# The self attention of a decoder block with its softmax normalised before the transposes

## The chip, the cores and the metric

The kernel runs on one core of a Trainium2 chip. The metric is the device time of one execution in microseconds; the time of a kernel is the median of its runs.

## The reference

One decoder layer on x (8 batches, 512 positions, 512 features), in fp32:

```python
x = x + attn(layernorm(x))          # this case: 16 heads of 64, causal, window 512, with scored global keys
x = x + cross_attn(ctx, layernorm(x), mask)
x = x + routed_ffn(layernorm(x))
# attn, h = rmsnorm(x) * norm_w:
q, k, v = h @ w_q, h @ w_k, h @ w_v
ll = where(causal, q k^T / 8, -1e30)               # local keys of the window
idx = top_k(h @ scorer_w + scorer_b, 128)          # global keys: their k and v are taken once more
lg = where(idx <= pos, q k[idx]^T / 8, -1e30)
a = softmax(concat(ll, lg)); o = a @ concat(v, v[idx]); return x + o @ w_out
```

As the window is the whole sequence, a chosen key counts twice in the softmax. The kernel never gathers: it ranks the scores and gives each chosen key the factor two.

## The kernel before

`self_attention` is one block with a program for each engine, and a loop over the 8 batches in each. The order of the work in a batch is a list written once by `attention_plan`; every engine walks it and does its own part of each entry, and semaphores carry the rest. So each engine's queue is in the order of the plan. Behind the self attention stand the cross attention and the feed-forward, which don't change.

A batch, in the plan's order. Each product of full precision is made of three products of rounded fp32 (high x high, low x high, high x low, `product`, L581 to L583).
- `v`: eight blocks of V = h w_v. ScalarE writes them to `vals` times `twice` (1 or 2 for each key, L381), and VectorE adds `twice` as a 65th column, so the values product also gives the row sum.
- `q`, `k`: a head pair's Q and K, 12 products of 512 columns each; ScalarE copies the high parts (Q once, K to both halves, L390 to L394), VectorE makes the low ones (L518, L522). Pair p + 1 is projected in the slots of pair p; pair 0 between the V blocks. All six weight parts stay in SBUF.
- Attention in slots g = 0 to 46. A head pair has five units of 512 score columns (`unit_blocks`). In slot g: `s` of unit g, `t` of unit g - 2, `pv` of unit g - 3.
- `s`: TensorE makes two score products and adds the causal mask with a bf16 product (L659 to L663) in one of two banks; VectorE takes the negated row maximum (L529, L534), ScalarE the exponential from PSUM to `probs` (L403).
- `t`: four fp32 transposes (L671), VectorE copies them to `probs_t` (L542).
- `pv`: fp32 products with the turned probabilities as the stationary operand and 65 columns of `vals` (L686, two passes each in the trace). VectorE inverts the row sum (L556) and scales the output (L557); `ot` transposes it (L695), ScalarE copies it to `o_t` (L411).
- `stats`, `dot`, `score`, `rank`: normalisation and ranking of the next batch, on VectorE and GpSimd; GpSimd's part (L323 to L337) makes scales from VectorE's statistics and scales `xb`. `ht`: `xb` turned for the next batch, after the last scores.
- `out`: four products of 8 fp32 matmuls (L710), each added to the residual on VectorE (L574) and stored. SP issues all loads and stores.

Ahead of the loop the weights are loaded in six parts of 1 MB in `W_ORDER`; ScalarE copies the high part (L366), VectorE subtracts for the low one (L481).

Of the kernel before, what the change touches and what calls it, by code (L numbers as in the profile page):

```python
# [18 lines left out]
F32 = mybir.dt.float32  # L19
# [5 lines left out]
ALU = mybir.AluOpType  # L25
# [59 lines left out]
def attention_plan():  # L85

    plan = [("v", i) for i in range(2 * TT - 2)] + [("q", 0), ("q_lo", 0), ("k", 0), ("k_lo", 0)]
    plan += [("v", i) for i in range(2 * TT - 2, 2 * TT)]
    for g in range(NU + 7):
        p, u = divmod(g, UNITS)
        if g < NU:
            plan.append(("s", g))
        if 2 <= g < NU + 2:
            plan.append(("t", g - 2))  # L100
        if 3 <= g < NU + 3:
            plan.append(("pv", g - 3))
        if g < NU and p + 1 < NPAIR and u < 4:
            plan.append((("q", "q_lo", "k", "k_lo")[u], p + 1))
        if g == 5:
            plan.append(("stats", 0))
        if g == 14:
            plan.append(("dot", 0))
        if g == 18:
            plan.append(("score", 0))  # L110
        if g in RANK_AT:
            plan.append(("rank", RANK_AT.index(g)))
# [14 lines left out]
def self_attention(nc, x, norm_w, w_q, w_k, w_v, w_out, scorer_w, scorer_b, x1):  # L127

    plan = attention_plan()
    PROJ, PT = bank_index(plan, ("v", "q", "k", "out")), bank_index(plan, ("t", "score", "ht", "ot"))  # L130
    with ExitStack() as ctx:
# [42 lines left out]
        twice = sb("twice", [P, TT])  # L174
        nmax = sb("nmax", [P, 4, 2])
# [70 lines left out]
        def _(sp):  # L246
# [1511 lines left out]
```

## Time and profile before

| | |
|---|---|
| time, median of 3 runs | 2299.57 us (2298.17 to 2301.93) |
| the profiled execution's own time | 2303.6 us |
| its span | 2301.9 us |
| mean granted TensorE clock | 0.945 of 2.4 GHz |
| TensorE busy | 2120.8 us, 92% |
| VectorE busy | 1320.5 us, 57% |
| ScalarE busy | 930.6 us, 40% |
| GpSimd busy | 343.7 us, 15% |

Busy times are of the whole span; the self attention takes the first two thirds of it. The profiled execution is one execution of the program, its span runs from the first to the last instruction. PE is TensorE, PEld its weight loads, DVE is VectorE, ACT ScalarE, POOL GpSimd, SP the engine that issues the DMAs. L574 is line 574 of the kernel before.

### The profile page before, as it was taken

What the parts mean: (1) busy time and instruction counts of PE and PEld (TensorE: products, weight loads), DVE (VectorE), ACT (ScalarE), POOL (GpSimd) and SP (SyncE); (2) the same over time, 40 slices, a digit from 0 to 9 for tenths busy, and PEclk for the clock granted to TensorE, in tenths of its full rate; (3) what the DMA queues carried; (4) which work ended last, traced back from release to release, by engine and by line L of the source; (5) the groups of instructions that cost most, each with busy time, mean ns of one, the idle gap of its engine ahead of it and who ended that gap; (6) DMA issues with size and microseconds to landing.
All of it is one profiled execution on the core that took longest, in us unless ns stands there. A gap on an engine that the chain in (4) does not pass through costs nothing. (4 is left out here: it accounts for less than half of the span.)

```text
span 2301.9 us, 36078 instructions
## 1 busy us (share of the span) xinstructions
PE 2120.8 (92%) x12029; PEld 1654.5 (72%) x12029; DVE 1320.5 (57%) x3145; ACT 930.6 (40%) x1989; POOL 343.7 (15%) x605
## 2 busy tenths in 40 slices
PE   3999999999999999999999999996899999978899
PEld 2886787688588688778868868864788888854543
DVE  5584376178167347537717826743787878745401
ACT  3442344244144244334415414424866666413210
POOL 2100100010010010001001001003554445320000
PEclk9999999999999999999999999996987878769899
DMA  5000000100100100000010010002013212150000
GB/s 192 1 2 33 24 1 13 44 1 1 56 1 1 55 3 1 27 31 1 11 47 1 1 57 1 1 33 81 27 59 133 61 58 67 51 201 1 1 0 19
DMA packets 46137, 80.24 MB, mean 35 GB/s; under 512 B 10067, under 2 KB 10067, under 8 KB 45448
## 3 DMA queue, kind: packets, MB, share of 16 engines
q1 hardware_dynamic: 45320, 75.85, 9.9%
q8 instruction: 103, 1.69, 0.3%
q0 software_dynamic: 640, 2.10, 0.2%
q14 instruction: 74, 0.61, 0.1%
HBM read 60.11 MB, written 17.83 MB: 34 GB/s over the span
## 5 line engine op out<-in xcount | busy, mean ns | idle before, releaser
L403 ACT ACTIVATE probs<-s_bank,nmax 128x512 f32<-128x512 f32 (+3 forms) x512 | 249.5, 526 | 368.5 <-DVE nmax L534 266.4
L686 PE MATMUL o_bank<-vals,probs_t 128*128 128x65 f32 x2560 | 329.0, 272 | 0.1
L686 PEld LDWEIGHTS o_bank<-vals,probs_t 128*128 128x128 f32 x2560 | 312.5, 192 | 13.1 <-DVE probs_t L542 12.9
L534 DVE TENSOR_REDUCE nmax<-s_bank 128x1 f32<-128x512 f32 (+2 forms) x384 | 184.4, 508 | 189.2 <-PE s_bank L663 186.5
L710 PE MATMUL pj_bank<-w_o,o_t 128*128 128x512 f32 x512 | 221.8, 594 | 6.0 <-ACT o_t L411 6.0
L542 DVE COPY probs_t<-pt_bank 128x512 f32<-128x512 f32 x320 | 217.8, 681 | 2.2 <-PE pt_bank L671 2.1
L671 PE MATMUL pt_bank<-ident,probs 128*128 128x128 f32 x1280 | 194.9, 275 | 15.7 <-DVE o_t L449 15.7
L659 PE MATMUL s_bank<-k_twice,q_both 128*128 128x512 f32 (+3 forms) x512 | 190.0, 373 | 2.1 <-DVE k_lo L522 2.1
L710 PEld LDWEIGHTS pj_bank<-w_o,o_t 128*128 128x128 f32 x512 | 96.6, 190 | 126.5 <-issue 126.5
L381 ACT ACTIVATE vals<-pj_bank,twice 128x512 f32<-128x512 f32 x64 | 43.9, 688 | 340.4 <-PE pj_bank L583 334.8
L518 DVE SCALAR_TENSOR_TENSOR q_both<-pj_bank,q_both 64x512 fp32r<-64x512 f32 x128 | 88.1, 688 | 141.7 <-ACT q_both L390 139.1
L661 PE MATMUL s_bank<-k_lo,q_both 128*128 128x512 f32 (+3 forms) x512 | 164.3, 321 | 0.0
L1255 PEld LDWEIGHTS x_o_bank<-vx,p_t 77*128 77x128 f32 x1024 | 148.0, 223 | 15.4 <-issue 5.4
L317 POOL TENSOR_TENSOR idle<-ones 128x4 f32<-128x4 f32 x41 | 8.1, 198 | 978.8 <-DMA probs<-in_x 976.7
L1071 ACT ACTIVATE e<-e,e_max 128x77 f32<-128x77 f32 x512 | 134.9, 351 | 33.3 <-DVE e_max L1130 33.3
L671 PEld LDWEIGHTS pt_bank<-ident,probs 128*128 128x128 f32 x1280 | 136.1, 142 | 16.5 <-issue 16.5
L1255 PE MATMUL x_o_bank<-vx,p_t 77*128 77x33 f32 x1024 | 143.4, 300 | 2.8 <-DVE att L1137 2.8
L574 DVE TENSOR_TENSOR probs<-pj_bank,probs 128x512 f32<-128x512 f32 x32 | 22.1, 691 | 212.1 <-PE pj_bank L710 199.8
L581 PE MATMUL pj_bank<-wv_hi,ht_hi 128*128 128x512 f32 x256 | 104.3, 407 | 22.8 <-ACT vals L381 9.9
L1020 POOL TENSOR_TENSOR e<-e,fill 128x616 f32<-128x616 f32 x64 | 95.4, 1491 | 187.3 <-DVE fill L1125 187.3
L663 PE MATMUL s_bank<-causal_b,ident_b 128*128 128x128 bf16 x512 | 118.0, 230 | 0.0
L1241 PE MATMUL e_bank<-qk_bd,xl_t 128*128 128x308 f32 x256 | 94.5, 499 | 23.3 <-DVE e L1119 22.6
(268 smaller groups left out, 4125.3 us busy)
## 6 DMA issues: line engine op xcount, KB each, us to landing
xb<-in_x SPq DMA_DIRECT2D x9, 1024.0 KB, 5.8
xt<-x SPq DMA_DIRECT2D x36, 256.0 KB, 2.8
probs<-in_x SPq DMA_DIRECT2D x32, 256.0 KB, 2.6
x<-probs SPq DMA_DIRECT2D x32, 256.0 KB, 2.0
am<-in_L_ffn_attention_mask SPq DMA_DIRECT2D x8, 1024.0 KB, 5.3
out<-x SPq DMA_DIRECT2D x32, 256.0 KB, 2.5
w_sb<-in_L_ffn_w SPq DMA_DIRECT2D x2, 4096.0 KB, 20.4
o_t<-in_L_attn_w_v SPq DMA_DIRECT2D x2, 1024.0 KB, 9.6
```

The costliest lines, as they stand in the source:

```text
L403: ins = nc.scalar.activation(probs[:, i % 2, c0:c0 + nk], s_bank[i % 2][:, c0:c0 + nk], ACT.Exp, bias=nmax[:, i % 4, n:n + 1])
L534: ins = nc.vector.tensor_reduce(nmax[:, i % 4, n:n + 1], s_bank[i % 2][:, c0:c0 + nk], AX.X, ALU.max, negate=True)
L542: nc.vector.tensor_copy(probs_t[:, i % 2, :], pt_bank[slot][:, :]).then_inc(ts_ready, 1)
L581: nc.tensor.matmul(out, lhs_hi, rhs_hi, start=start, stop=False)
L659: nc.tensor.matmul(s_bank[slot][:, c0:c0 + nk], both, k_twice[:, p % 2, h, 0:nk], start=True, stop=False)
L661: nc.tensor.matmul(s_bank[slot][:, c0:c0 + nk], both, k_lo[:, p % 2, h, 0:nk], start=False, stop=False)
L663: ins = nc.tensor.matmul(s_bank[slot][:, c0 + nk - P:c0 + nk], ident_b[:, :], causal_b[:, :], start=False, stop=True)
L671: ins = nc.tensor.transpose(pt_bank[slot][:, P * j:P * j + P], probs[:, i % 2, P * j:P * j + P], ident[:, :])
L686: ins = nc.tensor.matmul(o_bank[slot][:, o0:o0 + VW], probs_t[:, i % 2, c0 + P * kt:c0 + P * kt + P], vals[:, kt, 2 * p + h, :], start=(kt ...
L710: ins = nc.tensor.matmul(pj_bank[slot][:, :], o_t[:, c, P * i:P * i + P], w_o[:, c, :], start=(c == 0), stop=(c == NPAIR - 1))
L1071: ins = nc.scalar.activation(e[:, i % 4, h, :], e[:, i % 4, h, :], ACT.Exp, bias=e_max[:, i % 2, h:h + 1])
L1255: ins = nc.tensor.matmul(o_bank[:, VX * h:VX * h + VX], p_t[:, i % 2, h // CH, P * (h % CH):P * (h % CH) + P], vx[:, n.par, 2 * CH * (i % ...
```

## The change

The self attention is written anew in the same scheme of slots, three units to a head (512; 128 and 384; 256 columns), 48 units in a batch.
- Q is scaled by -1/8. VectorE adds a mask to the negated scores while it takes their minimum, and writes the sum to `probs`, a ring of four (`tensor_tensor_reduce`). The mask (`masks`, built once a batch by `build_masks` from a transposed row, entry `tw`) holds 1e30 for later keys and -ln 2 for chosen ones; the causal products and `twice` are gone.
- ScalarE takes the exponential from SBUF in place and accumulates the row sum (`den`). At the end of the next slot VectorE inverts it (`inverse`), and GpSimd multiplies the probabilities by it (`norm`); the transposes `t` are at g - 3.
- The turned probabilities are split: ScalarE copies the high part (`turned_hi`), VectorE subtracts for the low one (`turned_lo`). V is split in the same way, its low part beside the high one in `vals`.
- `pv`: once a head, eight products of rounded fp32 with 128 columns of `vals` (high and low) as the stationary operand and the turned probabilities as the moving one. The output comes out transposed; its two halves are added by a ScalarE copy (`o_raw`) and a VectorE addition (`o`). `ot` is gone.
- Projections of Q and K are cut in thirds of four products, one a slot; pair 0 of the next batch is projected in slots 50 to 55, `ht` moves to slots 46 to 49, `dot`, `score` and `rank` between the output products. `stats` is in slot 6.
- Split weights of Q and K no longer stay in SBUF: ahead of the loop SP stores them to device memory (`store_parts`), and each pair's 1 MB is loaded again per batch (`load_pair`). SP also moves K's high part to the other half by two DMAs (`move_k`), in place of ScalarE's copies.

Its core; removed lines stand in the functions above and are left out here:

```diff
+STEPS = (("o_raw", 8), ("k_high", 0), ("turned_hi", 3), ("norm", 1), ("s", 0), ("k_lows", 1), ("pv", 8), ("q_high", 0),
+         ("project", 0), ("q_low", 2), ("turned_lo", 4), ("t", 3), ("o", 9), ("inverse", 1))
+AHEAD, LAST_PAIR_AT, HT_AT, STATS_AT = 2, 50, 46, 6
...
+def unit_rows(u):
+    return ([(3, 0, 512)], [(0, 0, 128), (2, 128, 384)], [(1, 0, 256)])[u]
...
+thirds = {}
+for i in range(1, NPAIR + 1):
+    q0 = 2 * UNITS * (i - 1) - AHEAD if i < NPAIR else LAST_PAIR_AT
+    for j in range(3):
+        thirds[q0 + j] = ("q_third", 3 * i + j)
+        thirds[q0 + 3 + j] = ("k_third", 3 * i + j)
...
+plan = [("v", i) for i in range(2 * TT - 1)] + [("tw", 0), ("v", 2 * TT - 1)]
+for g in range(-AHEAD, LAST_PAIR_AT + 8):
+    for step, behind in STEPS:
+        n = g - behind
+        if step in ("norm", "s", "t", "turned_hi", "turned_lo", "inverse") and 0 <= n < NU:
+            plan.append((step, n))
+        if step in ("pv", "o_raw", "o") and n >= 0 and n % UNITS == 0 and n // UNITS < NH:
+            plan.append((step, n // UNITS))
+        if step == "project" and g in thirds:
+            plan.append(thirds[g])
+        if step in ("q_high", "q_low", "k_high", "k_lows") and last_third.get(n, " ")[0] == step[0]:
+            plan.append((step, last_third[n][1]))
...
+def store_parts(i):
+    n, hw = W_ORDER[i]
+    sp.wait_ge(split_lo, i + 1)
+    for part in range(2):
+        kind, r0 = 2 * (n == "k") + part, NPAIR // 2 * hw
+        if hw == 0:
+            for r in range(2):
+                sp.dma_start(w_pairs[r, :, kind, :], pair_part(i, r, part).rearrange("p c e -> p (c e)")
+                             .bitcast(F32)).then_inc(w_stored[i % 2], 16)
+        first = 2 if hw == 0 else 0
+        spare = (q_spare if i == 0 else p_spare)[part][:, DC * P * first:DC * P * (NPAIR // 2)]
+        sp.dma_start(w_pairs[r0 + first:r0 + NPAIR // 2, :, kind, :].rearrange("r p m -> p r m"),
+                     spare.rearrange("p (r m) -> p r m", m=DC * P).bitcast(F32)
+                     ).then_inc(w_stored[i % 2], 16)
...
+def move_k(b, i):
+    sp.wait_ge(k_hi_ready, i + 1 if b is None else b * NPAIR + i + 1)
+    for h in range(2):
+        own, other = head_rows(h), head_rows(1 - h)
+        sp.dma_start(k_twice[other, i % 2, h, :].bitcast(F32), k_twice[own, i % 2, h, :].bitcast(F32)
+                     ).then_inc(k_moved[i % 2], 16)
...
+def load_pairs(b, pairs):
+    for p in pairs:
+        if p > 2:
+            move_k(b, p - 2)
+        sp.wait_ge(k_low_ready, b * NPAIR + p - 1)
+        load_pair(p % NPAIR)
...
+if kind == "norm":
+    pl.wait_ge(den_ready, b * NU + i + 1)
+    for n, (_, c0, nk) in enumerate(unit_rows(i % UNITS)):
+        part = probs[:, i % RING, c0:c0 + nk]
+        ins = nc.gpsimd.tensor_tensor(part, part, rden[:, i % 4, n:n + 1].broadcast_to((P, nk)),
+                                      ALU.mult)
+    ins.then_inc(norm_ready, 1)
...
+if i == 3:
+    act.wait_ge(w_stored[0], STORED[0])
...
 if kind == "s":
     act.wait_ge(max_ready, b * NU + i + 1)
+    for n, (_, c0, nk) in enumerate(unit_rows(i % UNITS)):
+        part = probs[:, i % RING, c0:c0 + nk]
+        ins = nc.scalar.activation(part, part, ACT.Exp, bias=nmax[:, i % 4, n:n + 1], scale=-1.0,
+                                   accum_out=den[:, i % 4, n:n + 1])
     ins.then_inc(p_ready, 1)
+if kind == "turned_hi":
+    h, u = divmod(i, UNITS)
+    slot, ready = pt(b, ("t", i))
+    act.wait_ge(pt_ready, ready)
+    if u == 0 and h >= 2:
+        act.wait_ge(pv_ready, b * NH + h - 1)
+    n = len(TURN_ORDER[u])
+    nc.scalar.copy(p_hi[:, h % 2, TURNED_AT[u], :],
+                   pt_bank[slot][:, 0:P * n].rearrange("p (n k) -> p n k", k=P)).then_inc(hi_ready, 1)
...
+if kind == "o_raw":
+    act.wait_ge(pv_ready, b * NH + i + 1)
+    if i >= 2:
+        act.wait_ge(o_ready, b * NH + i - 1)
+    nc.scalar.copy(o_b[head_rows(i % 2), :], o_bank[i % 2][HD:P, :]).then_inc(ob_ready, 1)
...
+if i < 2:
+    dv.wait_ge(x1_out[i], b * (16 * TT // 2) + 1)
+elif i >= RING:
+    dv.wait_ge(pt_ready, pt(b, ("t", i - RING))[1])
+nc.vector.memset(carrier[:, 6 + i % 4:7 + i % 4], 0.0)
+m0 = MASK_AT[i % UNITS]
+for n, (_, c0, nk) in enumerate(unit_rows(i % UNITS)):
+    ins = nc.vector.tensor_tensor_reduce(
+        probs[:, i % RING, c0:c0 + nk], s_bank[i % 2][:, c0:c0 + nk],
+        masks[:, m0 + c0:m0 + c0 + nk], 1.0, 3e38, ALU.add, ALU.min, nmax[:, i % 4, n:n + 1])
 ins.then_inc(max_ready, 1)
...
+if kind == "inverse":
+    dv.wait_ge(p_ready, b * NU + i + 1)
+    n = len(unit_rows(i % UNITS))
+    nc.vector.reciprocal(rden[:, i % 4, 0:n], den[:, i % 4, 0:n]).then_inc(den_ready, 1)
+if kind == "turned_lo":
+    h, u = divmod(i, UNITS)
+    slot, _ = pt(b, ("t", i))
+    dv.wait_ge(hi_ready, b * NU + i + 1)
+    n = len(TURN_ORDER[u])
+    nc.vector.tensor_tensor(p_lo[:, h % 2, TURNED_AT[u], :],
+                            pt_bank[slot][:, 0:P * n].rearrange("p (n k) -> p n k", k=P),
+                            p_hi[:, h % 2, TURNED_AT[u], :].bitcast(F32),
+                            ALU.subtract).then_inc(lo_ready, 1)
+if kind == "o":
+    dv.wait_ge(ob_ready, b * NH + i + 1)
+    rows = head_rows(i % 2)
+    nc.vector.tensor_tensor(o_t[rows, i // 2, :], o_bank[i % 2][0:HD, :], o_b[rows, :],
+                            ALU.add).then_inc(o_ready, 1)
...
+def project(b, kind, i, thirds):
+    slot, _ = pj(b, (kind, i))
+    hi, lo = (w_qk[:, i % 2, 2 * (kind == "k") + k] for k in range(2))
+    for n in range(4 * thirds[0], 4 * thirds[-1] + 4):
+        c, form = divmod(n, 3)
+        w, moving = ((hi, ht_hi), (lo, ht_hi), (hi, ht_lo))[form]
+        ins = nc.tensor.matmul(pj_bank[slot][:, :], w[:, c, :], moving[:, c, :], start=(n == 0),
+                               stop=(n == 3 * DC - 1))
+    if thirds[-1] == 2:
+        ins.then_inc(pj_ready, 1)
...
 if kind == "s":
+    h, u = divmod(i, UNITS)
+    p = h // 2
+    if h % 2 == 0 and u == 0:
+        pe.wait_ge(q_lo_ready, b * NPAIR + p + 1)
+        pe.wait_ge(k_low_ready, b * NPAIR + p + 1)
+        pe.wait_ge(k_moved[p % 2], b * (32 * NPAIR // 2) + 32 * (p // 2 + 1))
     if i >= 2:
+        pe.wait_ge(max_ready, b * NU + i - 1)
+    for t, c0, nk in unit_rows(u):
+        both = q_both[:, p % 2, h % 2, P * t:P * t + P]
+        nc.tensor.matmul(s_bank[i % 2][:, c0:c0 + nk], both, k_twice[:, p % 2, h % 2, 0:nk],
                          start=True, stop=False)
+        ins = nc.tensor.matmul(s_bank[i % 2][:, c0:c0 + nk], both, k_low[:, p % 2, h % 2, 0:nk],
                                start=False, stop=True)
     ins.then_inc(s_ready, 1)
 if kind == "t":
     slot, _ = pt(b, (kind, i))
+    pe.wait_ge(norm_ready, b * NU + i + 1)
     pt_empty(b, (kind, i))
+    for j, k in enumerate(TURN_ORDER[i % UNITS]):
+        ins = nc.tensor.transpose(pt_bank[slot][:, P * j:P * j + P],
+                                  probs[:, i % RING, P * k:P * k + P], ident[:, :])
     ins.then_inc(pt_ready, 1)
 if kind == "pv":
     if i == 0:
+        pe.wait_ge(v_lo_ready, b * (2 * TT) + 2 * TT)
+    pe.wait_ge(lo_ready, b * NU + UNITS * i + UNITS)
     if i >= 2:
+        pe.wait_ge(o_ready, b * NH + i - 1)
+    parts = [(p, k) for p in (p_hi, p_lo) for k in (0, 3, 1, 2)]
+    for n, (part, k) in enumerate(parts):
+        ins = nc.tensor.matmul(o_bank[i % 2][:, 0:P * (TT - k)], vals[:, k, i, :],
+                               part[:, i % 2, KEYS_AT[k], :], start=(n == 0),
+                               stop=(n == len(parts) - 1))
     ins.then_inc(pv_ready, 1)
```

## Rows read from the trace of the kernel before

**Rows 1.** Windows view: length, busy time and count of each engine, granted clock, DMA.
```profile
422.10:451.20 29.10, 28.19 (x122) 22.66 (x122) 2.99 (x6) 8.39 (x14) 0.00 (x0) 1.00 0.15 46
451.20:583.20 132.00, 127.89 (x892) 110.06 (x890) 101.27 (x245) 63.02 (x119) 8.87 (x20) 0.99 0.01 5
478.97:495.15 16.18, 16.18 (x114) 13.90 (x113) 11.02 (x26) 7.88 (x15) 0.00 (x0) 1.00 0.00 2
```

**Rows 2.** Output additions (L574) of batch 0 and of batch 7.
```profile
L574 DVE TENSOR_TENSOR probs<-pj_bank,probs x4: 692/692/692, 212.8 to 233.3; 128x512 f32<-128x512 f32 x4
...
L574 DVE TENSOR_TENSOR probs<-pj_bank,probs x4: 691/691/691, 1532.6 to 1553.2; 128x512 f32<-128x512 f32 x4
```

**Rows 3.** TensorE's timeline, projections: start, duration, line; first and last of 95.
```profile
422.50 0.40 PE L582 MATMUL pj_bank<-wv_hi,ht_lo 128*128 128x512 f32 x1
...
443.83 0.39 PE L583 MATMUL pj_bank<-ht_lo,wk_hi 128*128 128x512 f32 x1
```

**Rows 4.** TensorE's timeline, two attention slots without a projection.
```profile
566.26 0.48 PE L659 MATMUL s_bank<-k_twice,q_both 128*128 128x512 f32 x1
566.57 0.40 PE L661 MATMUL s_bank<-k_lo,q_both 128*128 128x512 f32 x1
566.81 0.23 PE L663 MATMUL s_bank<-causal_b,ident_b 128*128 128x128 bf16 x1
566.88 0.60 PE L671 MATMUL pt_bank<-ident,probs 128*128 128x128 f32 x4
567.32 1.00 PE L686 MATMUL o_bank<-vals,probs_t 128*128 128x65 f32 x8
568.13 0.31 PE L659 MATMUL s_bank<-k_twice,q_both 128*128 128x128 f32 x1
...
568.43 0.42 PE L659 MATMUL s_bank<-k_twice,q_both 128*128 128x384 f32 x1
568.69 0.34 PE L661 MATMUL s_bank<-k_lo,q_both 128*128 128x384 f32 x1
568.87 0.23 PE L663 MATMUL s_bank<-causal_b,ident_b 128*128 128x128 bf16 x1
```

**Rows 5.** VectorE: two groups by form, and two steps of its timeline.
```profile
L522 DVE TENSOR_TENSOR k_lo<-pj_bank,k_twice 64x512 fp32r<-64x512 f32 x128 | 87.7, 685 | 22.7 <-ACT k_twice L394 19.9 <-issue 1.8
...
L556 DVE RECIPROCAL o_rden<-o_bank 128x2 f32<-128x2 f32 x192 | 31.3, 163 | 3.0 <-PE o_bank L686 2.0
...
498.15 0.69 DVE L440 SCALAR_TENSOR_TENSOR o_t<-xb,sw 128x512 f32<-128x512 f32 x1
...
498.89 0.69 DVE L440 SCALAR_TENSOR_TENSOR o_t<-xb,sw 128x512 f32<-128x512 f32 x1
```

**Rows 6.** ScalarE, the exponential's widest form.
```profile
L403 ACT ACTIVATE probs<-s_bank,nmax 128x512 f32<-128x512 f32 x128 | 88.2, 689 | 118.6 <-DVE nmax L534 110.4 <-PE pt_bank L671 3.3
```

**Rows 7.** GpSimd and VectorE side by side, timeline; and one line's durations (min/median/max).
```profile
16.58 2.29 DVE L481 TENSOR_TENSOR wv_lo<-o_t,wv_hi 128x2048 fp32r<-128x2048 f32 x1 [0.28 <-ACT wv_hi L366]
16.71 5.06 POOL L337 TENSOR_SCALAR xb<-xb,st 128x512 f32<-128x512 f32 x4
...
468.88 0.20 POOL L323 TENSOR_TENSOR st<-mv,eps_ln 128x4 f32<-128x4 f32 x1 [53.59 <-DVE mv L428]
...
473.89 3.03 POOL L337 TENSOR_SCALAR xb<-xb,st 128x512 f32<-128x512 f32 x4
...
1717.58 1.49 POOL L1020 TENSOR_TENSOR e<-e,fill 128x616 f32<-128x616 f32 x1 [6.53 <-DVE fill L1125]
1717.65 0.42 DVE L1137 TENSOR_TENSOR att<-x_o_bank,att_den 128x256 f32<-128x256 f32 x1
...
L1024 POOL TENSOR_TENSOR x<-xt,att x64: 721/730/1178, 1599.0 to 2000.8; 128x256 f32<-128x256 f32 x64
```

**Rows 8.** Before the first batch: ScalarE's timeline, and a load of weights (us to landing).
```profile
48.93 1.27 ACT L381 ACTIVATE vals<-pj_bank,twice 128x512 f32<-128x512 f32 x2 [5.62 <-DVE wk_lo L481]
...
o_t<-in_L_attn_w_q SPq DMA_DIRECT2D x2, 1024.0 KB, 5.1
```

More of the change, by code:

```diff
@@ L117, in attention_plan @@
-    plan.append(("ot", NPAIR - 1))
-    plan += [("out", t) for t in range(TT)]
+    thirds = {}
[4 more added lines that the diff above has]
+            thirds[q0 + 3 + j] = ("k_third", 3 * i + j)
+    last_third = {g: (kind[0], n // 3) for g, (kind, n) in thirds.items() if n % 3 == 2}
+    plan = [("v", i) for i in range(2 * TT - 1)] + [("tw", 0), ("v", 2 * TT - 1)]
@@ L124, in bank_index, with self_attention @@
     return {s: i for i, s in enumerate([s for s in plan if s[0] in kinds])}
-def self_attention(nc, x, norm_w, w_q, w_k, w_v, w_out, scorer_w, scorer_b, x1):
+def self_attention(nc, x, norm_w, w_q, w_k, w_v, w_out, scorer_w, scorer_b, w_pairs, x1):
     plan = attention_plan()
-    PROJ, PT = bank_index(plan, ("v", "q", "k", "out")), bank_index(plan, ("t", "score", "ht", "ot"))
+    PROJ = bank_index([(kind[0], i // 3) if kind.endswith("third") else (kind, i) for kind, i in plan
+                       if not kind.endswith("third") or i % 3 == 2], ("v", "q", "k", "out"))
+    PT = bank_index(plan, ("t", "score", "ht", "tw"))
     with ExitStack() as ctx:
@@ L182, in self_attention @@
         w_loaded, split_hi, split_lo = [sem(f"w_loaded{i}") for i in range(2)], sem("split_hi"), sem("split_lo")
+        w_stored, pair_in = [sem(f"w_stored{i}") for i in range(2)], [sem(f"pair_in{i}") for i in range(2)]
         small_in, wo_in, x_in = sem("small_in"), sem("wo_in"), sem("x_in")
@@ L464, in rank, with build_masks @@
                     step(nc.vector.tensor_tensor(cnt[:, 0, :], cnt[:, 0, :], cnt[:, 1, :], ALU.add))
-                    if b is not None:
-                        dv.wait_ge(v_ready, n * (2 * TT))
-                    nc.vector.tensor_scalar(twice[:, :], cnt[:, 0, :], TOPK - 0.5, 1.0, ALU.is_lt,
-                                            ALU.add).then_inc(twice_ready, 1)
+                    nc.vector.tensor_scalar(chosen[:, :], cnt[:, 0, :], TOPK - 0.5, -LN2, ALU.is_lt,
+                                            ALU.mult).then_inc(chosen_ready, 1)
+            def build_masks(b):
+                slot, ready = pt(b, ("tw", 0))
+                dv.wait_ge(pt_ready, ready)
+                row = pt_bank[slot]
+                for at, n in ((0, 3), (640, 2), (1024, 1)):
+                    done.mark(nc.vector.tensor_copy(masks[:, at:at + P * n], row[:, 0:P * n]))
+                for at, k in ((384, 3), (512, 0), (896, 2), (1152, 1)):
+                    ins = nc.vector.tensor_tensor(masks[:, at:at + P], row[:, P * k:P * k + P], later_keys[:, :], ALU.add)
+                done.wait(dv)
+                ins.then_inc(masks_ready, 1)
             def normed(b, n, c):
@@ L623, in _ @@
                 transposed(None, 0, c)
+            pe.wait_ge(ht_lo_ready, DC)
+            pe.wait_ge(split_lo, 1)
+            project(None, "q", 0, range(3))
+            pe.wait_ge(split_lo, 2)
+            project(None, "k", 0, range(3))
             score_rows(None, 0)
```

432 lines of the change are left out of this document (206 added, 226 removed).

## The prediction

> **What bounds the kernel now.** I read the windows view over one batch of the self attention first. The projection of V takes 29.1 us, the attention stretch 132.0 us, and in the latter TensorE is busy 127.9 us, VectorE 101.3, ScalarE 63.0 and GpSimd 8.9; over one head pair of 16.18 us TensorE is never free and VectorE is busy 11.0 [rows 1]. So TensorE's own issue order sets the time. The period of a batch follows from the first output addition of batch 0 at 212.8 and of batch 7 at 1532.6: 1319.8 / 7 = 188.5 us [rows 2]. The eight periods end near 1554 us; the cross attention and the feed-forward behind them, 748 us, are not touched by the diff. Then I took the prices of TensorE's work from its timeline: 94 steps of a 512-wide product from 422.50 to 443.83, so 0.227 us each or 0.443 ns a column [rows 3]; and one slot without projection, 1.87 us: scores 0.62 (the last 0.07 is the causal product), four transposes 0.44, probabilities by values 0.81 [rows 4].
>
> **What the change removes from TensorE.** Per head, after: score products 1.5 us (the same 2 x 1280 columns; 0.31 + 0.24 for the 512-wide pair, 0.26 for the 128-wide one, 0.45 for the 384-wide one, 0.33 estimated for 256 [rows 4]); ten transposes at 0.11, 1.1 us, as before; the values product as eight products of 512, 128, 384, 256 columns twice, 2560 x 0.443 ns = 1.13 us, and 1.3 with the 128-wide ones costing 0.13 more than their columns [rows 3, 4]; projections 12 x 0.227 = 2.7 us. Sum 6.65 us a head, 13.3 a pair, against 16.18 [rows 1]. Gone are the causal products (some 0.2 a head), 0.7 of 2.05 us on the values product, and the transposes of the output.
>
> **What it adds to VectorE.** Durations end to start overlap a little, so I use spacings. The masked minimum (a two-input operation that reads PSUM and a mask and returns a row value) is in no row. Its lower bound is a plain pass, 0.61 us for 512 columns, the upper one two cycles an element, +0.53 us on 512; the nearest row is the multiply with an accumulated sum, 0.74 us from start to start [rows 5]. I take that: 0.74, 0.34, 0.61 and 0.47 for 512, 128, 384, 256 columns, 2.16 a head (1.95 to 3.5). Three memsets and three reciprocals 0.6 (the reciprocal is 0.16 [rows 5]); the low parts of the turned probabilities 0.65 + 0.65 + 0.39 = 1.7, like any 512-wide pass; the output addition 0.7; the low parts of Q and K 1.4 a head, as now (0.685 each, [rows 5]). Sum 6.55 us a head. VectorE goes from 68% of the pair to 98% of TensorE's new 6.65: the two are level, and what I predict hangs on that.
>
> **ScalarE and GpSimd.** ScalarE takes over the high copies of the turned probabilities (1.3 us a head) and the upper half of the output (0.5) beside the exponentials (2.1 at 0.69 for 512 columns [rows 6]) and two copies of Q and K a head (1.0). The accumulated row sum is shown nowhere on ScalarE; nothing to 0.2 us for each of four, I take 0.1. About 5.3 us a head, 80%, covered by TensorE. The normalisation on GpSimd: 616 columns take 1.49, 256 take 0.73 [rows 7], so 1.28, 1.5 and 0.77 us for the three units, 3.6 a head. It waits for the reciprocal at the end of VectorE's next slot and is wanted at the end of TensorE's slot three: more than a slot (2.2 us) of room, so free, except in one place.
>
> That place is slot 6. VectorE takes the next batch's statistics there (2.9 us now), and GpSimd then works them off, 468.88 to 476.92, 8.0 us with the four scalings that begin at 473.89 [rows 7]. Now nothing is behind that in GpSimd's queue; afterwards the normalisation of unit 6 is, then 7 and 8. In slots from the first third: TensorE ends slot 5 at 11.4, VectorE starts slot 6 at 12.0 and ends it with the statistics at 16.2; GpSimd is free at 24.3, unit 6 is normalised at 25.7, its transposes end at 26.2 instead of 19.9. TensorE can do nothing else in between: 6.3 us a batch lost. The granted clock is 1.00 and 0.99 of the upper level in these stretches [rows 1]; what such a stall does to it no row of them shows, and I leave it to the range.
>
> **Port.** VectorE's subtraction with both inputs in SBUF, 2.29 us at 16.58 ran beside GpSimd's four scalings, which took 5.06 us; four of the same at 473.89 took 3.03, with no such operation beside them. At 1717.58 GpSimd's product took its usual 1.49 us while VectorE ran a PSUM-and-SBUF product of 0.42 [rows 7]. The added VectorE work is of this last form, so I add nothing. The Trainium skill (SBUF — State Buffer, "SBUF: two separate sides") says that GpSimd and VectorE share a port pair as an exclusive lock, taken by a VectorE operation with two SBUF inputs; by this rule the added operations, with one input in PSUM, don't collide, and the trace agrees. Read more broadly, as if any two-input operation took the lock, the rule would give the last rival below.
>
> **One batch.** Fill and the statistics, to the end of slot 9: 26.2 us. Slots 10 to 39, five pairs, at 13.3 plus 3% for waits between two level engines, 13.7: 68.5. Slots 40 to 47 have no projection; VectorE sets them, 8/3 x 5.15 = 13.7, less 0.9 that TensorE is ahead. Slots 48 on: turned probabilities and the next batch's transposes alternate in two banks and each waits for ScalarE and VectorE, 2 x 2.3, then the last products and six thirds of a projection, 8.3: 12.9. Sum 120.4. The V stage is 96 x 0.227 = 21.8, with the wait for the last addition 0.9 and one row of transposes for the mask 0.45: 23.2. The first Q and K, 5.4 us of it now, have moved into the slots. The output products stay 27.5. Together 171.1 against 188.5: 17.4 us a batch, 139 in eight.
>
> **Before the first batch.** ScalarE's first copy of V starts at 48.93 and waits for the last weight split [rows 8]. Now the weights are written to memory in between: the fifth part is split until some 43.8, its store of 2 MB (5.1 us for 1 MB [rows 8], so 7.5 estimated) lands at 51.5, the last part is copied and split in 5.2 us, to 56.5, and its store holds ScalarE until 64. That is 15 us later. SP carries more too: two SBUF-to-SBUF moves and a 1 MB load a pair. The move of K is issued some 1.1 us after the last third's end and is wanted 4.8 us after that slot. No row shows such a move: the 1 MB load at 5.1 us [rows 8] is its upper bound, and up to 3.7 us it fits. I take it as fitting; at the bound it costs 1.4 us in seven pairs, 10 us a batch. Behind it in SP's queue stand only the next pair's load, wanted 14 us later, and at the end of a batch the stores of the output.
>
> **The sum.** Profiled execution 2303.6 (span 2301.9 and 1.7 around it) + 15 - 139 = 2180; the median of the runs is 4 us under the profiled one, so 2176.
>
> **Rivals.**
> - *TensorE alone sets the time*: statistics fit in, no loss at slot 9. Batch 164.8, 8 x 23.7 = 190 off, 2125. For it: the other engines' sums are all below 6.65. Against it: GpSimd's queue is in order. Chance 0.15.
> - *Waits between the engines*: the K move lands late, or row sums on ScalarE cost 0.2 each, and a pair takes 15.0. Six to eight such pairs make 7.5 us a batch: 2236. For it: four engines hand each unit on, at 80 to 98% each. Chance 0.22.
> - *Slower, through the masked minimum*: at two cycles an element VectorE needs 6.55 + 1.33 = 7.9 us a head, 21.3 more a batch, 192.4 in all: +31 + 15, 2346. It decides from where the batch has lost 15.5 us, 1.0 a head or 0.25 us on each such operation. For it: no row shows it. Against it: accumulating rows run at one element a cycle. Chance 0.13.
> - *GpSimd and VectorE exclude each other*: 3.5 us a head more, 56 a batch, about 2620. The product at 1717.58 speaks against it. Chance 0.04.
> - *The bound isn't where I see it, no change*: 0.03.
>
> My forecast has 0.43; its own range is 2140 to 2215. 0.2% (4.6 us) is about what a measurement of this kernel tells from no change. Faster 0.80, within 0.03, slower 0.17. From the first rival to beyond the second the range is 2110 to 2270.
>
> **What would show it.** A period between first output additions of 170 to 172 us; TensorE's steady pair at 13.3 to 13.9 with VectorE over 93% busy; one idle stretch of TensorE of 4 to 7 us a batch, released by GpSimd, some 20 us after the V stage; masked minimum 0.69 to 0.77 us for 512 columns; the normalisation 1.2 to 1.35; ScalarE's first copy of V near 64. I am wrong if VectorE's minimum is above 1 us, if GpSimd's products are longer than 1.5 us at 512 columns, or if the score products wait for the K move in each pair.

## The result, and the profile after

The changed kernel takes 2241.03 us (median of 4 runs, 2240.01 to 2247.91) against 2299.46 for the kernel before, measured beside it: a ratio of 0.9751, with an interval of 0.9730 to 0.9772. It is faster, by 58 us; 123 were forecast. Its profiled execution spans 2238.0 us.

The page of the changed kernel: span, busy time by engine, granted clock in 40 slices.

```profile
span 2238.0 us, 34486 instructions
...
PE 1966.6 (88%) x9781; PEld 1515.5 (68%) x9781; DVE 1410.7 (63%) x4171; ACT 1114.9 (50%) x2837; POOL 705.8 (32%) x1116
...
PEclk9899999999999999999999999988888878678899
```

The output additions (L716 now) of batch 0 and batch 7, which answer to [rows 2]:

```profile
L716 DVE TENSOR_TENSOR probs<-pj_bank,probs x4: 690/691/692, 221.5 to 242.5; 128x512 f32<-128x512 f32 x4
...
L716 DVE TENSOR_TENSOR probs<-pj_bank,probs x4: 691/692/692, 1468.5 to 1489.5; 128x512 f32<-128x512 f32 x4
```

The period is (1468.5 - 221.5) / 7 = 178.1 us; it was 188.5 and should have become 171.1. So 10.4 us a batch came in and 7.0 are missing, 56 of the 60 us between the profiled execution (2240.0) and its forecast (2180). Of the rest, 2.6 are in front: the first copy of V starts at 66.63, not 64. The medians lie 65 us apart, not 60, because the forecast took off 4 us from the profiled execution to its median, and this one lies 1 us below its median. The stretch behind the eight periods is 748 us long, as before.

The windows view of batch 2, which answers to [rows 1]: V; slots to 8; slot 9 with a stall; the three slots behind it; slots to 39; 40 to 46; the tail to the first output product; the output. The last line is one steady head pair. Columns: length; busy time and count of PE, PEld, DVE, ACT, POOL; clock; DMA share; GB/s.

```profile
421.50:443.80 22.30, 22.26 (x100) 18.46 (x101) 6.43 (x14) 4.11 (x7) 0.00 (x0) 1.00 0.32 107
443.80:461.90 18.10, 17.49 (x96) 14.61 (x95) 14.46 (x58) 12.54 (x33) 6.84 (x11) 1.00 0.23 74
461.90:470.50 8.60, 2.73 (x14) 2.12 (x13) 4.02 (x12) 2.99 (x8) 7.73 (x17) 0.82 0.13 31
470.50:478.20 7.70, 7.70 (x36) 6.62 (x35) 4.55 (x16) 4.33 (x12) 3.00 (x5) 0.76 0.41 134
478.20:536.40 58.20, 58.20 (x348) 50.64 (x347) 52.75 (x184) 48.78 (x127) 25.49 (x36) 1.00 0.29 92
536.40:549.00 12.60, 9.73 (x62) 7.31 (x60) 11.99 (x48) 11.77 (x33) 6.27 (x10) 1.00 0.35 105
549.00:571.00 22.00, 16.29 (x81) 13.61 (x82) 9.48 (x19) 9.16 (x19) 4.69 (x8) 0.84 0.07 25
571.00:599.10 28.10, 27.11 (x67) 11.88 (x65) 13.97 (x34) 0.41 (x1) 2.28 (x6) 1.00 0.18 58
...
484.67:497.50 12.83, 12.83 (x78) 11.15 (x77) 11.61 (x41) 10.78 (x28) 5.66 (x9) 1.00 0.32 104
```

The steady pair is better than forecast: 12.83 us, TensorE never free. The time is lost at its two ends, around 465 and from 536 on. TensorE's waits say for what:

```profile
PE pt_bank L835 <- DVE p_lo L693: 59.8, 40, 2.3
PE pt_bank L835 <- POOL probs L435: 48.8, 16, 5.9
```

Each row gives a total in us, how often, and the longest. The second is the stall that was forecast at 6.3 us a batch. Its timeline in batch 2:

```profile
465.54 3.02 POOL L420 TENSOR_SCALAR xb<-xb,st 128x512 f32<-128x512 f32 x4
468.52 2.75 POOL L435 TENSOR_TENSOR probs<-probs,rden 128x512 f32<-128x512 f32 x4
469.61 1.11 PE L835 MATMUL pt_bank<-ident,probs 128*128 128x128 f32 x4 [5.87 <-POOL probs L435]
470.38 0.46 PE L825 MATMUL s_bank<-k_twice,q_both 128*128 128x128 f32 x1
```

GpSimd scales the next input, then normalises the units that have piled up, and TensorE has stood for 5.87 us. The four transposes behind it take 1.11 us where they take 0.60 to 0.66 in the steady slots, and the granted clock over the next 7.7 us is 0.76: it starts at the lower level, 1.2 GHz (0.50), and is 1.00 again from 475.0 on.

The first row of waits was not in the forecast as such. A stretch of the tail, timeline of four engines:

```profile
552.29 0.41 PE L835 MATMUL pt_bank<-ident,probs 128*128 128x128 f32 x2 [1.10 <-DVE p_lo L693]
552.54 0.60 PE L753 MATMUL pt_bank<-ident,xb 128*128 128x128 f32 x4
552.74 0.37 ACT L517 CAST p_hi<-pt_bank 128x256 fp32r<-128x256 f32 x1 [0.94 <-PE pt_bank L835]
553.51 0.68 ACT L451 ACTIVATE ht_hi<-pt_bank,nw 128x512 fp32r<-128x512 f32 x1
554.22 0.75 DVE L596 SCALAR_TENSOR_TENSOR ht_lo<-pt_bank,nw,ht_hi 128x512 fp32r<-128x512 f32 x1 [2.00 <-ACT ht_hi L451]
554.88 0.41 DVE L693 TENSOR_TENSOR p_lo<-pt_bank,p_hi 128x256 fp32r<-128x256 f32 x1
555.44 0.63 PE L835 MATMUL pt_bank<-ident,probs 128*128 128x128 f32 x4 [2.31 <-DVE p_lo L693]
```

The input of `p_lo` (`p_hi`) was there at 553.11, but `ht_lo` of the slot before stands ahead of it in VectorE's queue and waits for ScalarE until 554.19. Only then is `p_lo` made, and TensorE gets its bank back at 555.4.

### The profile page after: what moved, and what is told of

Its sections match the earlier page's. It is cut to its first block and busy times, and to the rows that moved or that the text cites. A ratio compares the mean times of both kernels' runs of the same rounds, so it can differ in the third digit from the quotient of the medians.

```text
span 2238.0 us, 34486 instructions
## 1 busy us (share of the span) xinstructions
PE 1966.6 (88%) x9781; PEld 1515.5 (68%) x9781; DVE 1410.7 (63%) x4171; ACT 1114.9 (50%) x2837; POOL 705.8 (32%) x1116
## 5 line engine op out<-in xcount | busy, mean ns | idle before, releaser
L435 POOL TENSOR_TENSOR probs<-probs,rden 128x512 f32<-128x512 f32 (+3 forms) x512 | 361.5, 720 | 733.1 <-DVE rden L687 732.1
L775 PE MATMUL pj_bank<-ht_hi,w_qk 128*128 128x512 f32 x1040 | 351.5, 402 | 1.6 <-DVE ht_lo L596 1.6
L507 ACT ACTIVATE probs<-probs,nmax 128x512 f32<-128x512 f32 (+3 forms) x512 | 286.6, 562 | 26.3 <-DVE nmax L680 26.0
L517 ACT CAST p_hi<-pt_bank 128x512 fp32r<-128x512 f32 (+1 forms) x384 | 197.3, 514 | 195.5 <-PE pt_bank L835 191.4
L680 DVE CUSTOM_DVE_ANT_0 probs<-s_bank,masks 128x512 f32<-128x512 f32 (+3 forms) x512 | 240.5, 488 | 10.4 <-issue 10.1
L693 DVE TENSOR_TENSOR p_lo<-pt_bank,p_hi 128x512 fp32r<-128x512 f32 (+1 forms) x384 | 229.7, 598 | 17.9 <-ACT p_hi L517 14.7
L775 PEld LDWEIGHTS pj_bank<-ht_hi,w_qk 128*128 128x128 f32 x1040 | 198.8, 194 | 32.7 <-DVE ht_lo L596 2.0
L775 PE MATMUL pj_bank<-ht_lo,w_qk 128*128 128x512 f32 x520 | 207.8, 400 | 0.0
L827 PE MATMUL s_bank<-k_low,q_both 128*128 128x512 f32 (+3 forms) x512 | 167.3, 327 | 0.0
L723 PE MATMUL pj_bank<-wv_hi,ht_hi 128*128 128x512 f32 x256 | 102.1, 399 | 32.9 <-DVE vals L660 23.1
L660 DVE TENSOR_TENSOR vals<-pj_bank,vals 128x512 fp32r<-128x512 f32 x64 | 44.1, 691 | 135.4 <-ACT vals L497 135.4
```

Source lines behind the costliest of these rows:

```text
L435: ins = nc.gpsimd.tensor_tensor(part, part, rden[:, i % 4, n:n + 1].broadcast_to((P, nk)), ALU.mult)
L507: ins = nc.scalar.activation(part, part, ACT.Exp, bias=nmax[:, i % 4, n:n + 1], scale=-1.0, accum_out=den[:, i % 4, n:n + 1])
L517: nc.scalar.copy(p_hi[:, h % 2, TURNED_AT[u], :], pt_bank[slot][:, 0:P * n].rearrange("p (n k) -> p n k", k=P)).then_inc(hi_ready, 1)
L680: ins = nc.vector.tensor_tensor_reduce(probs[:, i % RING, c0:c0 + nk], s_bank[i % 2][:, c0:c0 + nk], masks[:, m0 + c0:m0 + c0 + nk], 1.0, ...
L693: nc.vector.tensor_tensor(p_lo[:, h % 2, TURNED_AT[u], :], pt_bank[slot][:, 0:P * n].rearrange("p (n k) -> p n k", k=P), p_hi[:, h % 2, TU ...
L775: ins = nc.tensor.matmul(pj_bank[slot][:, :], w[:, c, :], moving[:, c, :], start=(n == 0), stop=(n == 3 * DC - 1))
```

## Experiments

Each kernel's ratio is to the kernel before, run on the same chip; the brackets are 95% intervals. Differences from the changed kernel are against 2241.

**The two halves of the stall at slot 9.** e1 takes the statistics of the next input (VectorE's and GpSimd's part) out of slot 6 and puts them between blocks of V:

```diff
-    plan = [("v", i) for i in range(2 * TT - 1)] + [("tw", 0), ("v", 2 * TT - 1)]
+    plan = [("v", i) for i in range(2 * TT - 4)] + [("stats", 0)] + [("v", i) for i in range(2 * TT - 4, 2 * TT - 1)]
+    plan += [("tw", 0), ("v", 2 * TT - 1)]
...
-        if g == STATS_AT:
-            plan.append(("stats", 0))
```

> The statistics of the next batch (VectorE's part and GpSimd's) move from slot 6 into the V stage, behind the fourth V block. If GpSimd's queue order is what holds TensorE in slot 9, the 5.9 us wait and the some 2 us of half clock behind it go in each of eight batches: about 63 us off the changed kernel's 2241, 2178. If the waits have another source (VectorE level with TensorE), TensorE waits elsewhere and no more than 20 us go.

Measured 2177.64, ratio 0.9462 [0.9429, 0.9495]: 63 us faster than the changed kernel, 7.9 a batch, as expected. Of TensorE's 48.8 us of waits for GpSimd at the transposes 1.8 are left, and in batch 2 TensorE works without a gap from 444 to 456 us, in slot 9 (its scores start at 445.06) and behind it, at a clock of 1.00; the waits for `p_lo` stay, 59.9 us. e2 moves VectorE's half alone; GpSimd's part stays in slot 6.

```diff
+    plan = [("v", i) for i in range(2 * TT - 4)] + [("bn", 0)] + [("v", i) for i in range(2 * TT - 4, 2 * TT - 1)]
...
-                    if kind == "stats":
+                    if kind == "bn":
                         stats(b + 1)
```

> Only VectorE's statistics move into the V stage; GpSimd's 8 us of work on them stays in slot 6, ahead of the normalisation. If GpSimd's queue is the cause, its work starts some 3 us earlier and the wait of 5.9 us shrinks to about 3: 25 to 35 us off 2241. If VectorE's 2.9 us in slot 6 is the cause, this gives the whole gain of the run before it, about 63 us.

Measured 2225.4, ratio 0.9675 [0.9644, 0.9706]: 16 faster, less than the 25 to 35 expected; the stall shrinks from 5.9 to 3.7 us. So the larger part, the other 48 us of e1, hangs on GpSimd's 8 us in its queue, as forecast. In e1 47.0 us of waits went and 63 were gained: the difference, 2.0 us a batch, I read as the lower clock behind the stall.

**The tail: placement or queue order.** e3 starts the turning of the next input six slots earlier, into slots where TensorE has no projections.

```diff
-AHEAD, LAST_PAIR_AT, HT_AT, STATS_AT = 2, 50, 46, 6
+AHEAD, LAST_PAIR_AT, HT_AT, STATS_AT = 2, 50, 40, 6
```

> The four transposes of the next batch's input (with their high and low copies) move from slots 46 to 49 to slots 40 to 43. If the long tail comes from input transposes and probability transposes alternating in two banks while VectorE's queue holds them behind each other, the last slots shorten: 3 to 5 us a batch, 25 to 40 us off 2241. If VectorE's work is the bound from slot 40 on, as it is 95% busy there, what is saved in the tail comes back in slots 40 to 43: within 8 us.

Measured 2253.42, ratio 0.9815 [0.9772, 0.9858]: 12 slower than the changed kernel, and my theory of it fell. TensorE's waits for `p_lo` at its transposes stayed, 61.1 us, 21.7 instead of 10.3 came at the input's transposes, and its waits for GpSimd rose from 48.8 to 56.8. Earlier was no use by itself. e5 leaves the place and changes only VectorE's order: `ht_lo` one slot later, behind that slot's `turned_lo`.

```diff
+        if HT_AT + 1 <= g <= HT_AT + DC:
+            plan.append(("ht_lo", g - HT_AT - 1))
...
-                    if kind == "ht":
+                    if kind == "ht_lo":
                         normed(b, b + 1, i)
```

> The changed kernel with one thing moved: VectorE writes the low part of the next batch's turned input (ht_lo) one slot later, behind that slot's turned_lo; TensorE's and ScalarE's parts stay where they are. Theory (in VectorE's queue turned_lo stands behind the ht_lo of the slot before, which waits for ScalarE, so that TensorE waits twice per slot for its two transpose banks): slots 46 to 50 fall from 3.3 to 3.6 us each to about 2.5, TensorE's 59.8 us of waits for p_lo at L835 halve, 3 to 5 us a batch, 2200 to 2217. Rival (the tail is long because the chain of transposes, ScalarE and VectorE is long whatever the order, at half the clock): within 8 us of 2241.

Measured 2205.09, ratio 0.9569 [0.9533, 0.9604]: 36 faster than the changed kernel, at the fast end of the expectation. TensorE's waits in e5; slots 40 to 47 of batch 2, and from there to the first output product, in e5; and the same two stretches of the changed kernel:

```profile
PE pt_bank L755 <- DVE ht_lo L598: 16.5, 25, 0.9
PE pt_bank L837 <- DVE p_lo L695: 16.4, 24, 1.2
```

```profile
527.53:543.81 16.28, 13.03 (x83) 9.84 (x81) 14.23 (x55) 14.30 (x39) 8.60 (x13) 1.00 0.25 82
543.81:557.06 13.25, 10.94 (x60) 8.81 (x60) 7.36 (x13) 5.97 (x12) 2.47 (x5) 1.00 0.13 40
```

```profile
536.29:553.13 16.84, 12.82 (x83) 9.88 (x81) 13.87 (x54) 13.96 (x38) 8.26 (x13) 1.00 0.26 79
553.13:570.04 16.91, 12.35 (x59) 10.68 (x59) 7.70 (x13) 6.32 (x12) 2.82 (x6) 0.80 0.09 31
```

The same work takes 4.2 us less, 3.7 of them behind slot 47, where the clock is 1.00 instead of 0.80. Queue order is the cause of this part of the tail. e6 joins both edits.

> The edit of e5 and that of e3 together: the next batch's input is turned in slots 40 to 43, its low part one slot later on VectorE. If the queue's order made e3 12 us slower than the changed kernel, this is faster than e5: slots 40 to 43 have no projections on TensorE, so its work of 2.9 us fits there and leaves the tail, 2180 to 2205. Rival (VectorE, at nine tenths in the slots with scores, has no room for four operations of 0.75 us there): 2225 to 2250.

Measured 2238.7, ratio 0.9717 [0.9689, 0.9745], in the rival's range: TensorE's waits for `p_lo` rise from 16.4 to 32.8 us, and from 10.3 to 21.7 at the input's transposes. The rival's reason, that VectorE has no room beside the minima, its trace doesn't bear out. The window from the first to the last of the four input transposes of batch 2, and a piece of its timeline:

```profile
541.25:552.60 11.35, 7.40 (x38) 6.28 (x39) 6.51 (x21) 4.70 (x10) 3.71 (x5) 0.80 0.26 92
```

```profile
547.97 0.58 ACT L519 CAST p_hi<-pt_bank 128x512 fp32r<-128x512 f32 x1 [1.08 <-PE pt_bank L837]
...
550.15 0.06 DVE L679 MEMSET carrier<- 128x1 f32 x1 [1.44 <-PE s_bank L829]
...
550.89 0.69 DVE L695 TENSOR_TENSOR p_lo<-pt_bank,p_hi 128x512 fp32r<-128x512 f32 x1
...
551.72 1.09 PE L837 MATMUL pt_bank<-ident,probs 128*128 128x128 f32 x4 [1.72 <-DVE p_lo L695]
```

VectorE is busy 6.51 of the 11.35 us. `p_lo` could have been made from 548.72 on, when `p_hi` was there and VectorE free, but it stands behind the next minima, which wait 1.44 us for TensorE's scores; TensorE then waits for its bank, at a clock of 0.80 over the window. That is again an order of the queue and not VectorE's load. It is read from the trace; no run tests it.

**Is VectorE level with TensorE?** e7 adds a memset of 128 columns ahead of each masked minimum, 48 a batch, into an unused tile; e9 adds there a copy of 184 columns of the scores.

```diff
                         nc.vector.memset(carrier[:, 6 + i % 4:7 + i % 4], 0.0)
+                        nc.vector.memset(load[:, i % 4, :], 0.0)
```

```diff
                         nc.vector.memset(carrier[:, 6 + i % 4:7 + i % 4], 0.0)
+                        nc.vector.tensor_copy(load[:, i % 3, :], s_bank[i % 2][:, 0:184])
```

> The changed kernel with a memset of 128 columns of an unused tile added on VectorE before each masked minimum, 48 a batch, estimated at 0.12 us each from the 0.059 of one column. By the prediction's step (VectorE 98% full and level with TensorE) every one is paid: 48 x 0.12 = 5.8 us a batch, 46 in all, 2280 to 2290. By the trace of the changed kernel (VectorE 90% full in the steady pairs, 1.2 us of 12.8 free, 0.7 us added a pair) only slots 40 to 47 pay, about 1 us a batch: 2245 to 2258.

> The changed kernel with a larger load on VectorE than in e7: before each masked minimum it also copies 184 columns of the scores from the bank into an unused tile, about 0.35 us each (estimated from p_lo's 0.42 for 256 columns and 0.69 for 512), 48 a batch, 16.6 us. In a steady pair that is 2.07 us where 1.22 of 12.83 were free, so VectorE becomes the bound: 0.85 a pair for five pairs, and 2.8 in slots 40 to 47, where nothing is free, 7 to 8 a batch: 2295 to 2310. If every copy is paid (VectorE level with TensorE, the prediction's step): 133 more, 2370 or above. If VectorE has far more room than the busy share says: within 15 of 2241.

e7: 2241.32, ratio 0.9729 [0.9696, 0.9763], nothing, below both of its ranges. It says little, as it loaded VectorE less than planned: a memset took 0.165 us by the trace, but a steady pair holds 11.87 us of VectorE's work instead of 11.61. e9: 2267.68, ratio 0.9832 [0.9800, 0.9864], 27 slower, under half of what I expected from the busy share (54 to 69) and a fifth of what a level VectorE would cost (133). Why, the timeline of VectorE and the window of a steady pair in e9 show:

```profile
497.59 0.68 DVE L695 TENSOR_TENSOR p_lo<-pt_bank,p_hi 128x512 fp32r<-128x512 f32 x1
498.19 0.15 DVE L689 RECIPROCAL rden<-den 128x2 f32<-128x2 f32 x1
498.32 0.06 DVE L678 MEMSET carrier<- 128x1 f32 x1
498.32 0.35 DVE L679 COPY load<-s_bank 128x184 f32<-128x184 f32 x1
498.59 0.68 DVE L682 CUSTOM_DVE_ANT_0 probs<-s_bank,masks 128x512 f32<-128x512 f32 x1
499.19 0.08 DVE L682 DVE_READ_ACCUMULATOR2_ANT nmax<- 128x1 f32 x1
499.19 0.42 DVE L695 TENSOR_TENSOR p_lo<-pt_bank,p_hi 128x256 fp32r<-128x256 f32 x1
```

```profile
497.44:510.27 12.83, 12.83 (x78) 11.15 (x76) 12.65 (x47) 10.78 (x28) 5.68 (x9) 1.00 0.33 106
```

An operation of 0.68 us is followed by the next after 0.60, the copy of 0.35 by the next after 0.27. With six copies, 1.6 us more work in spacings (1.04 more in busy time, which counts overlaps once), the pair still takes 12.83 us, at 12.65 of VectorE. So in the steady pairs VectorE had room for 1.6 us more, where the forecast gave it 0.2. The 27 us of e9 come in elsewhere; at slot 42 of its batch 2, where there are no projections, TensorE waits 1.51 us for `p_lo`.

**GpSimd's distance.** e10 stands on e8 (below) and turns the probabilities two slots behind the scores instead of three, with everything after it one slot earlier.

```diff
-STEPS = (("o_raw", 8), ("k_high", 0), ("turned_hi", 3), ("norm", 1), ("s", 0), ("k_lows", 1), ("pv", 8), ("q_high", 0),
-         ("project", 0), ("q_low", 2), ("turned_lo", 4), ("t", 3), ("o", 9), ("inverse", 1))
+STEPS = (("o_raw", 7), ("k_high", 0), ("turned_hi", 2), ("norm", 1), ("s", 0), ("k_lows", 1), ("pv", 7), ("q_high", 0),
+         ("project", 0), ("q_low", 2), ("turned_lo", 3), ("t", 2), ("o", 8), ("inverse", 1))
```

> e8 with the probabilities' transposes, and all that follows them, one slot earlier: transposes 2 slots behind the scores (not 3), the products with V 7 (not 8). GpSimd's product has then only the time between the end of VectorE's slot and TensorE's transposes at the end of the next. If it fits (a slot of 2.14 us, a product of 1.04): one slot less before each output stage, 1 to 2.5 us a batch, 2120 to 2132. Rival (inverse and product, about 1.5 us with their hand-overs, do not fit): TensorE waits for GpSimd in each slot, 0.3 us or more, 48 a batch: above 2240.

Measured 2369.45, ratio 1.0289 [1.0246, 1.0331]: slower than the kernel before, 229 us above e8. The rival held. TensorE's row of waits, and two such waits in one pair:

```profile
PE pt_bank L836 <- POOL probs L436: 159.6, 132, 2.5
```

```profile
512.04 0.66 PE L836 MATMUL pt_bank<-ident,probs 128*128 128x128 f32 x4 [1.75 <-POOL probs L436]
517.51 0.66 PE L836 MATMUL pt_bank<-ident,probs 128*128 128x128 f32 x4 [0.64 <-POOL probs L436]
```

The pair takes 15.72 us (first scores at 502.21 and 517.93) instead of 12.83. GpSimd is 30% busy in this run; it is its place in the chain that costs, and VectorE has a part in it: ahead of the second of these waits the row sum was there at 514.03, VectorE's reciprocal came at 516.18, and the product of 1.04 us followed at 516.42. Of the 229 us, 160 are these waits; the mean clock of the self attention is 0.94 instead of 0.98, and the rest I did not follow up. e11 adds to e10 the turning of the next input and the last pair's projections, both one slot earlier.

```diff
-AHEAD, LAST_PAIR_AT, HT_AT, STATS_AT = 2, 50, 46, 6
+AHEAD, LAST_PAIR_AT, HT_AT, STATS_AT = 2, 49, 45, 6
```

> e10 with the turning of the next input (46 to 45) and the last pair's projections (50 to 49) one slot earlier too. If e10's earlier transposes fit, this gives the last slot back as well, 10 us below e10: 2105 to 2125. Rival (VectorE has no room for ht_lo beside the minima, as in e6): within 5 of e10 or above it.

Measured 2355.92, ratio 1.0212 [1.0178, 1.0247]: 13.5 better than e10, within neither of its expectations; e12 below tells that this is not to be had where TensorE doesn't wait for GpSimd.

**Ahead of the loop, and the best version.** e4 lets ScalarE wait for the last store of split weights only at its first `turned_hi`, not ahead of the loop.

```diff
-            act.wait_ge(split_lo, len(W_ORDER))
-            act.wait_ge(w_stored[1], STORED[5])
...
                         if u == 0 and h >= 2:
                             act.wait_ge(pv_ready, b * NH + h - 1)
+                        if i == 0:
+                            act.wait_ge(w_stored[1], STORED[5])
```

> ScalarE no longer waits ahead of the loop for the last weight store and split; it waits for the store only ahead of the first turned probabilities. ScalarE's first copy of V should start near 57 instead of 66.6 us: 10 us off 2241, once. If the V stage is held by something else there (VectorE's ranks), 3 us or less.

Measured 2236.44, ratio 0.9731 [0.9700, 0.9763], 5 faster, between its two expectations and not clear of noise by these intervals; in the traces TensorE's one long wait in this stage falls from 23.1 to 16.8 us. ScalarE's first copy of V comes at 56.63 instead of 66.63, but VectorE, still ranking, takes V up at 62.77 only. e8 joins e1, e4 and e5.

> Three edits together: e1 (both halves of the next input's statistics in the stage of V), e4 (ScalarE's wait for the stored weights put off) and e5 (ht_lo one slot later). If they add up: 2177.6 of e1, less 5 of e4, less what e5 gives, 24 to 40: 2133 to 2149. If e5 gives nothing: 2168 to 2177.

Measured 2140.26, ratio 0.9289 [0.9258, 0.9320]: the gains add up (63 + 5 + 36 = 104 expected from the single runs, 101 measured). It is the fastest of all, and 36 us below the forecast. e12 is e8 with e11's edit of `HT_AT` and `LAST_PAIR_AT`.

> e8 with the turning of the next input and the last pair's projections one slot earlier (45 and 49), the transposes left where they are. e11 was 13.5 us below e10 by this same edit; if it carries over, 2126 to 2135. Rival (there it only filled TensorE's waits for GpSimd, which e8 has not; VectorE is full in slot 45): 2137 to 2150.

Measured 2163.12, ratio 0.9396 [0.9370, 0.9423], 23 slower than e8, worse than its rival's range. TensorE's waits for `p_lo` double from 16.3 to 33.4 us; I read it as in e6. VectorE isn't full there (busy 10.17 of the 14.40 us from 517.60 to 532.00 in batch 2), and it stands 0.85 us for scores with a `p_lo` behind them whose input is there, while TensorE waits 1.73 us for that `p_lo`.

## Why the prediction came out as it did

Direction and place of the stall were right; the size was not. 2241 lies outside the forecast's own range of 2140 to 2215 and only inside the wide one, 2110 to 2270. By its own steps, for one batch:

- **TensorE's sum held.** 6.65 us a head forecast, 6.41 measured; the pair 12.83. (The four prices given for the scores add up to 1.6 us, not 1.5.)
- **"The two are level, and what I predict hangs on that" was wrong.** The masked minimum was priced by the nearest row at 0.74, 0.61, 0.47 and 0.34 us for 512, 384, 256 and 128 columns. The changed kernel's spacings are:

```profile
484.10 0.69 DVE L680 CUSTOM_DVE_ANT_0 probs<-s_bank,masks 128x512 f32<-128x512 f32 x1
484.72 0.08 DVE L680 DVE_READ_ACCUMULATOR2_ANT nmax<- 128x1 f32 x1
484.72 0.42 DVE L693 TENSOR_TENSOR p_lo<-pt_bank,p_hi 128x256 fp32r<-128x256 f32 x1
...
486.26 0.55 DVE L680 CUSTOM_DVE_ANT_0 probs<-s_bank,masks 128x384 f32<-128x384 f32 x1
486.74 0.08 DVE L680 DVE_READ_ACCUMULATOR2_ANT nmax<- 128x1 f32 x1
```

  0.62 for 512 and 0.48 for 384, so the minimum is a plain pass, the lower bound in the text. VectorE is at 90% of the pair (98% forecast), and e9 shows that even 12.65 of 12.83 us costs nothing there. The 3% added for level engines was not due: slots 10 to 39 took 2.6 us less than forecast, the slow slots after the stall included.
- **The stall of 6.3 us is confirmed**, in its place and cause: slot 9 ends at 470.5, 26.7 us after the slots begin, against 26.2. What it does to the clock was left to the range and not in the sum. From the transposes at 469.61 to those three slots later, at 478.24, 8.6 us pass instead of 6.4; the granted clock is 0.50 until 473.5 and 1.00 from 475.0. By e1 the whole is 7.9 a batch, not 6.3.
- **The mis-sized term is the end of the slots**, priced at 12.8 + 12.9 = 25.7 us. It took 33.6, from 536.4 to the first output product at 570.04: 7.9 us more, which is more than all that is missing. In that step I let each of the two banks wait "for ScalarE and VectorE", 2 x 2.3, as if VectorE took its work as it came. It takes it in the plan's order, so `p_lo` waited behind an `ht_lo` that waited for ScalarE, in slots of 3.4 to 4.0 us (from one turning of the input to the next). e5 takes 4.5 of the 7.9 away with that order alone, and with it the lower clock. The other 3.4 lie in slots 40 to 47: the stretch behind them takes 13.3 us in e5, against 12.9, but they still take 16.3, against 12.8. That price was VectorE's sum, 13.7, less a lead of 0.9. VectorE is busy 14.2 us there, with the first input turnings of slots 46 and 47, which the price left out; it stands idle for 2.1, and the lead isn't seen. TensorE's longest waits there are 1.20 and 1.29 us, for `p_lo`. Why VectorE is idle there no run separates.
- **ScalarE and GpSimd.** The row sum costs ScalarE an instruction of 0.191 us, of which about 0.1 is not hidden in the next, as taken. GpSimd's products are 1.04, 0.827 + 0.400 and 0.613 us, 2.9 a head, not 3.6. Neither decides in the steady pairs. But the room given for GpSimd, "more than a slot", was needed: e10 takes one slot away and loses 229 us.

```profile
L435 POOL TENSOR_TENSOR probs<-probs,rden 128x512 f32<-128x512 f32 x128 | 133.1, 1040 | 502.8 <-DVE rden L687 502.8
...
L507 ACT ACTIVATION_READ_ACCUMULATOR probs<-probs,nmax 128x1 f32 x512 | 97.8, 191 | 0.0
```

- **Ahead of the loop.** 66.63 against 64, the wait for the store as forecast:

```profile
66.63 1.07 ACT L497 CAST vals<-pj_bank 128x512 fp32r<-128x512 f32 x2 [9.77 <-DMA w_pairs<-p_lo]
```

- **The rivals.** *Slower, through the masked minimum* and *GpSimd and VectorE exclude each other* are excluded by the rows above. *Waits between the engines* gave the nearest number, 2236, but by another way: its mechanism was 15.0 us in the steady pairs, through K's move or the row sums, and these took 12.83; TensorE's waits for the K move are under 0.5 us in all, the move taking 2.3 us. *TensorE alone* is right for the steady pairs and wrong for both ends.

In all, a batch: +0.5 at slot 9, -2.6 for slots 10 to 39 (65.9), +7.9 for the end of the slots, and +1.2 for V and the output together (178.1 - 126.2 = 51.9, priced at 50.7), which I did not follow up: the 7.0 us that are missing. The two errors work against each other: the steady pairs were priced too long and the end of the slots too short, so it is luck that no more than 7.0 are missing.

## What to carry to other kernels

When two chains share an in-order engine, write down for each wait what stands behind it in that queue: `p_lo`, ready, cost 36 us behind an `ht_lo` that was not, and putting it first was a matter of one entry in the plan. Price the ends of a software pipeline slot by slot, as the steady state is; there the chain between engines sets the pace. An engine that is 30% busy stood in a chain that cost 229 us when its step got one slot too few. Add to a stall what TensorE's clock does behind it, and for VectorE add up spacings, not durations.

## What the runs showed of the hardware

- VectorE's durations overlap at their ends by some 0.08 us: 0.68 long and 0.60 apart, 0.42 and 0.33, 0.35 and 0.27. The Trainium skill (Perfetto Trace Analysis, "DVE / Act Engine Instruction (TENSOR_ADD, Activation, etc)") has a profiled instruction end at the acknowledgement of its writes, while the next may already start its reads; the trace agrees.
- A 128-column memset took 0.165 us by the trace, and 384 of them added nothing to the time: the minimum behind it starts 0.08 us after it and is about 0.06 us shorter (632 ns instead of 691 for 512 columns).
- A masked minimum over a row from PSUM costs a plain pass (0.62 us from start to start for 512 columns, `p_lo`'s pass 0.60); the read of its accumulator (0.083 us) lies wholly under the next instruction. ScalarE's (0.191 us) does so only by half.
- After 5.9 us in which TensorE stood, its transposes ran at the lower clock level, 1.11 us for four instead of 0.60 to 0.66. In the tail of the changed kernel TensorE stood 1.29, 1.10 and 2.31 us, working in between; the granted clock was 1.00 until 556, 0.53 from 556 to 558 and 0.50 until 562, and 1.00 again from 563. With waits of 1.3 us at most, in e5, the clock of that stretch was 1.00.
